# Zeroing the last blocks in 21 calls, and dense products in column groups, in a four-layer graph network on one core

## The chip, the cores and the metric

The kernel runs on one NeuronCore of a Trainium2 chip. The metric is the device time of one execution in microseconds. Before the change three executions gave a median of 3755.14 us (3753.14 to 3758.54).

The engines are TensorE (PE in the profile, with its weight loads as PEld), VectorE (DVE), ScalarE (ACT), GpSimd (POOL) and SyncE (SP, which starts most transfers). Sixteen DMA engines move the data.

## The reference

There are N = 6250 nodes with 128 features and E = 100000 edges. Four graph layers follow each other, each followed by a residual sum and a layer norm. All is float32.

```
agg0 = segment_sum(edge_attr, src) / max(count, 1)
x = layernorm(x + three_dense_layers_with_relu_and_batchnorm([x, agg0, u]))
x = layernorm(x + relu((segment_sum(x[src], dst) / max(deg, 1) + x) @ W1 + b1))
msg = [x[src], x[dst]] @ Wmsg[edge_type] + bmsg[edge_type]
h = [x, segment_sum(msg, dst) / max(count, 1)] @ Wupd + bupd
x = layernorm(x + (x + gelu(layernorm(h) * gamma2 + beta2)))
out3 = segment_sum(norm * (x @ W3)[row], col) + b3     # with self loops
x = layernorm(x + batchnorm(relu(out3)))
```

The two dense products of this study are `(agg + x) @ W1` of the second layer (layer 1) and `agg @ Wupd[128:]` of the third (layer 2).

## The kernel before

**Sorting the edges into blocks.** The nodes are cut into 49 groups of 128, so an edge belongs to one of 49 x 49 = 2401 pairs of groups. The kernel gives each pair blocks of four slots in a DRAM table, `slots`; a slot has 136 floats (128 features and 8 of payload), a block 544 floats, 2176 bytes. The last block of each pair may be part empty, so it is zeroed first. For this VectorE makes the list of the 2401 last blocks (`last_b`, 49 x 49), SyncE writes it to DRAM and reads it back as a table with one row to a lane, `zero_idx` (L556 to L561), and GpSimd issues 19 indirect transfers of zeros (L734), each with one column of the table, 128 lanes. Lanes without an entry hold a number out of bounds, and write nothing.

GpSimd then waits until all the zeros have landed, and scatters the edges: 782 indirect transfers (L750) of 128 edges each, 544 bytes to an edge. While it does that, TensorE, VectorE and ScalarE work out where each edge goes.

**The layers.** After the sort the kernel reads the slots back (`reduce`), gathers source rows (`gather`) and scatters them again, layer by layer. Each layer's sums over edges are matmuls with one-hot matrices (L1379, L1412, L1414, L1424). Between these long loops stand short stages on the nodes, in STEPS = 7 steps of STEP = 7 groups.

**The two stages of this study** are `f1` (layer 1) and `f2` (layer 2). A step of either goes in a ring over three engines. VectorE makes seven 128 x 128 operands in `zr` (L2065, L2141); TensorE turns them with seven transposes into PSUM (`turn`, L1465); ScalarE copies them to `zt` (L1004); TensorE multiplies each of the seven by the weights (`dense`, L1521); VectorE takes the products (L2072 and L2074 in `f1`, L2148 in `f2`). One PSUM area (banks 2 and 3) holds the products, so `dense` of a step waits until VectorE has taken those of the step before, and ScalarE's copy to `zt` waits for the `dense` before it. The program order on TensorE is written out by hand: turn of step i + 1, then dense of step i. In the second half of `f1`, TensorE does the messages of layer 2 between these steps (L1538, L1541).

In `dense` the turned nodes are the stationary operand (128 x 128) and the weights the moving one (128 columns). Each float32 matmul stands in the trace as two weight loads and two matmul records; a transpose stands as one of each.

Of the kernel before, what the change touches and what calls it, by code (L numbers as in the profile page):

```python
# [16 lines left out]
P = 128  # L17
# [7 lines left out]
STEPS = GROUPS // STEP  # L25
# [22 lines left out]
BLK = 4  # L48
# [70 lines left out]
ROW_A = D + PAY  # L119
ROW_G = D + 6  # L120
AW = D + 5
NOWHERE = 1.0e6
LASTB = 19
LASTP = GROUPS * GROUPS // LASTB
LASTN = GROUPS * GROUPS - LASTP * LASTB
assert LASTP < P and 0 < LASTN

HALF = STEP * P // 2
EPS = 1e-5
# [51 lines left out]
def gnn_kernel(nc, x, src, dst, edge_attr, edge_type, edge_weight, u, W0, b0, W1, b1, W2, b2,  # L181
               g0, bt0, g1, bt1, g2, bt2, L1W, L1b, Wmsg, bmsg, Wupd, bupd, gam2, bet2,
               W3, b3, gam3, bet3, out):
    with ExitStack() as ctx:
        def sb(name, shape, dt=F32):
            return ctx.enter_context(nc.sbuf_tensor(name, shape, dt))
# [4 lines left out]
        def dram(name, shape, dt=F32):  # L191
            return nc.dram_tensor(name, shape, dt).ap()

        slots = dram("slots", [NBLK, BLK * ROW_A])
# [14 lines left out]
        zt = sb("zt", [P, STEP, D])  # L209
# [73 lines left out]
        zeros = hot_raw[:, 0:BLK * BLK * ROW_A]  # L283
# [28 lines left out]
        last_b = sb("last_b", [GROUPS, GROUPS], U32)  # L312
        zero_idx = sb("zero_idx", [P, LASTB], U32)
        key_bc = pays_raw[:, COLS * PAY:COLS * PAY + ARING * CB * P // 2].bitcast(I16).rearrange(
# [35 lines left out]
        wT = sb("wT", [P, 6, D])  # L350
        wcat = sb("wcat", [P, 8, D])
# [100 lines left out]
        def tslot(j, base=0):  # L452
            return ps[:, base + j // 4, (j % 4) * D:(j % 4 + 1) * D]
# [40 lines left out]
        def turned_keys(k):  # L494
            return ps[0:KROWS, 3 + k, 0:CB * P // 2].bitcast(BF16).rearrange("p (q n) -> p q n", q=CB)
# [11 lines left out]
        def _(sp):  # L507
# [44 lines left out]
            for k, v in enumerate((bmsg[0], bmsg[1], bmsg[2], bupd, L1b)):  # L552
# [5 lines left out]
            flat = last_blocks.rearrange("a b -> (a b)")  # L558
            sp.dma_start(zero_idx[0:LASTP, :], flat[0:LASTP * LASTB].rearrange("(p k) -> p k", k=LASTB)).then_inc(
                last_out, 16)  # L560
            sp.dma_start(zero_idx[LASTP:LASTP + 1, 0:LASTN], flat[LASTP * LASTB:].rearrange(  # L561
                "(p k) -> p k", k=LASTN)).then_inc(last_out, 16)
# [127 lines left out]
        def _(pool):  # L690
# [39 lines left out]
            pool.sem_inc(issued, 1)  # L730
            pool.wait_ge(last_out, 48)
            pool.sem_inc(issued, 1)
            for k in range(LASTB):
                pool.indirect_dma_start(  # L734
                    slots, bass.IndirectOffsetOnAxis(zero_idx[:, k:k + 1], 0), zeros[:, 0:BLK * ROW_A], None,
                    bounds_check=NBLK - 1, oob_is_err=False).then_inc(last_zero, 16)
            pool.wait_ge(last_zero, 16 * LASTB)
            pool.sem_inc(issued, 1)
# [507 lines left out]
        def _(pe):  # L1246
# [14 lines left out]
            for k in range(2):  # L1261
                for q in range(CB):
                    ins = pe.transpose(turned_keys(k)[:, q, :], sg[:, k, q * KROWS:(q + 1) * KROWS], ident_h[:, :])
# [8 lines left out]
            for c in range(2):  # L1272
                ins = pe.matmul(ps[0:GROUPS, 7, 256:256 + GROUPS], ident[0:PAIR, c:PAIR:2], pair_sums[:, c:PAIR:2],
                                start=c == 0, stop=c == 1)
# [5 lines left out]
                      stop=True).then_inc(tables_turned, 1)  # L1280
# [50 lines left out]
            for k in range(2):  # L1331
                n = min(4, VECTORS - 4 * k) * D
                if k:
                    pe.wait_ge(prep_out, 6 + k)
                pe.matmul(bank(7, n), ones[0:1, :], bc_src[0:1, 4 * k * D:4 * k * D + n],
                          start=True, stop=True).then_inc(prep_t, 1)
# [20 lines left out]
            for k, b in ((0, 5), (1, 1)):  # L1357
                pe.matmul(bank(b, TILES), row128[0:GROUPS, 0:1].broadcast_to([GROUPS, P]), tile_on[:, k, :],
                          start=True, stop=True)
                pe.matmul(bank(b + 1, TILES), heads[:, 8 + k:9 + k].broadcast_to([GROUPS, P]), tile_on[:, k, :],  # L1360
                          start=True, stop=True)
                pe.matmul(bank(b + 2, TILES), ones[0:GROUPS, :], tile_on[:, k, :],
                          start=True, stop=True).then_inc(tile_done, 1)
# [97 lines left out]
            def turn(stage, i, operands=zr, base=0):  # L1461

                for j in range(STEP):
                    pe.wait_ge(st[stage]["z"], i * STEP + (j + 1))
                    ins = pe.transpose(tslot(j, base), operands[:, j, :], ident[:, :])  # L1465
                ins.then_inc(st[stage]["t"], 1)
# [24 lines left out]
            for k, stage in ((1, "mlp1"), (2, "mlp2")):  # L1491
                for n in range(2 * STEPS):
                    pe.wait_ge(bn_applied, (k - 1) * 2 * STEPS + n + 1)
                    pe.matmul(product_bank(stage, n), wT[:, 2 + k, :], A[:, n * HALF:(n + 1) * HALF],
                              start=True, stop=True).then_inc(st[stage]["m"], 1)
                if k == 1:
                    pe.wait_ge(lanes_ready, 3)
                    for v, table in enumerate((lanes, lanes_t)):
                        if v:
                            pe.wait_ge(lane_rows_made, v)  # L1500
                        for q in range(LTURNS):
                            ins = pe.transpose(lanes_turned[:, q, :], table[:, q * LCOLS:(q + 1) * LCOLS], ident_h[:, :])
# [11 lines left out]
            gather(1)  # L1514
            reduce(1)

            def dense(stage, w, i):

                pe.wait_ge(st[stage]["c"], i + 1)
                for j in range(STEP):  # L1520
                    ins = pe.matmul(tslot(j, 2), zt[:, j, :], w, start=True, stop=True)  # L1521
                ins.then_inc(st[stage]["m"], 1)


# [25 lines left out]
            def f1_dense(i):  # L1550
                if i:
                    pe.wait_ge(st["f1"]["r"], i)
                dense("f1", wT[:, 5, :], i)

            turn("f1", 0)
            f1_turn(1)
            f1_dense(0)
            f1_turn(2)
            f1_dense(1)
            f1_turn(3)  # L1560
            f1_dense(2)

            f1_dense(3)
# [28 lines left out]
            turn("f2", 0)  # L1592
            pe.wait_ge(st["f2"]["c"], 1)
            turn("f2", 1)
            dense("f2", wcat[:, 7, :], 0)
            with pe.Fori(1, STEPS - 1) as i:
                pe.wait_ge(st["f2"]["c"], i + 1)
                turn("f2", i + 1)
                pe.wait_ge(st["f2"]["r"], i)
                dense("f2", wcat[:, 7, :], i)  # L1600
            pe.wait_ge(st["f2"]["r"], STEPS - 1)
            dense("f2", wcat[:, 7, :], STEPS - 1)

            def z_turn(i):
                if i < CHUNKS[2][0]:
# [637 lines left out]
```

## Time and profile before

| | |
|---|---|
| median of the runs | 3755.14 us (3753.14 to 3758.54) |
| span of the profiled execution | 3754.1 us (the profile has no other time of that execution; the span lies 1.0 us under the median) |
| mean granted TensorE clock | 0.961 |
| busy: PE, DVE, POOL, ACT | 75%, 67%, 50%, 40% |
| chain that ended last | PE 39%, POOL 23%, issue 14%, DMA 12%, DVE 5%, ACT 3% |

In the chain, "issue" is time in which an engine waited for nothing that the profile shows. The share of busy time is a mean over stages that have different limits: GpSimd carries the chain while it scatters the edges (114 to 1103 us), TensorE in most of the rest. The stages `f1` (2063 to 2134 us, shared with the messages of layer 2) and `f2` (2999 to 3043 us) are short.

### The profile page before, as it was taken

What the parts mean: (1) busy time and instruction counts of PE and PEld (TensorE: products, weight loads), DVE (VectorE), ACT (ScalarE), POOL (GpSimd) and SP (SyncE); (2) the same over time, 40 slices, a digit from 0 to 9 for tenths busy, and PEclk for the clock granted to TensorE, in tenths of its full rate; (3) what the DMA queues carried; (4) which work ended last, traced back from release to release, by engine and by line L of the source; (5) the groups of instructions that cost most, each with busy time, mean ns of one, the idle gap of its engine ahead of it and who ended that gap; (6) DMA issues with size and microseconds to landing.
All of it is one profiled execution on the core that took longest, in us unless ns stands there. A gap on an engine that the chain in (4) does not pass through costs nothing.

```text
span 3754.1 us, 95326 instructions
## 1 busy us (share of the span) xinstructions
PE 2826.7 (75%) x23184; PEld 2448.4 (65%) x23185; DVE 2500.2 (67%) x7099; ACT 1518.9 (40%) x4337; POOL 1873.3 (50%) x2268
## 2 busy tenths in 40 slices
PE   8555544444439986778799799999999957777996
PEld 6232322222229965777799479999888957777995
DVE  7666666666647778555577777777666776554667
ACT  0111000000004445555576543222365347887665
POOL 4777777777763342777434344444432007774000
PEclk9999999999999998999899899999999969998998
DMA  6444444444449933888697035555477817786883
GB/s 214 151 149 144 146 149 141 149 143 147 148 130 290 291 128 118 279 275 277 221 290 255 9 127 180 173 183 177 136 226 235 263 38 269 275 275 197 286 281 122
DMA packets 419029, 721.55 MB, mean 192 GB/s; under 512 B 68624, under 2 KB 198169, under 8 KB 417932
## 3 DMA queue, kind: packets, MB, share of 16 engines
q1 hardware_dynamic: 330492, 494.35, 43.0%
q0 software_dynamic: 88464, 226.43, 16.0%
q14 instruction: 52, 0.43, 0.0%
q8 instruction: 21, 0.34, 0.0%
HBM read 481.26 MB, written 285.09 MB: 204 GB/s over the span
## 4 chain that ended last, share of the span: by engine, by line
PE 39%; POOL 23%; issue 14%; DMA 12%; DVE 5%; ACT 3%; SPq 2%; DVEq 1%; POOLq 1%; ACTq 0%
POOL slots L750 19%; PE ps L1379 18%; PE ps L1412 9%; DMA gbuf<-ring_raw,to_blk 8%; PE ps L1414 5%; POOL gbuf L804 4%; DMA ring_raw<-gbuf 3%; PE ps L1254 2%; PE ps L1465 1%; PE ps L1456 1%; SPq L501 1%; SPq L622 1%; DVE stats L1930 1%; PE ps L1521 1%; DVEq L501 1%
## 5 line engine op out<-in xcount | busy, mean ns | idle before, releaser
L804 POOL DMA_INDIRECT gbuf<-ring_raw,to_blk x774 | 754.2, 974 | 728.9 <-DVE ring_raw L1863 261.9
L750 POOL DMA_INDIRECT slots<-ring_raw,idx_edges x782 | 751.4, 961 | 242.3 <-issue 242.3
L1379 PE MATMUL ps<-ring_raw,memory 128*128 128x128 f32 (+2 forms) x6576 | 783.9, 279 | 84.9 <-DVE memory L1831 49.4
L1379 PEld LDWEIGHTS ps<-ring_raw,memory 128*128 128x128 f32 x6576 | 763.3, 192 | 113.1 <-issue 60.3
L1831 DVE TENSOR_TENSOR memory<-dst_lane,lane_ids 128x512 f32<-128x512 f32 x774 | 539.6, 698 | 73.3 <-POOL dst_lane L768 51.1
L1290 PE MATMUL ps<-memory 128*49 128x343 bf16 (+6 forms) x784 | 263.5, 489 | 387.9 <-DVE memory L1727 386.6
L1412 PE MATMUL ps<-memory 128*128 x2752 | 497.7, 273 | 10.2 <-DVE memory L1872 8.0
L1841 DVE TENSOR_TENSOR memory<-memory,ps 128x128 f32 (+2 forms) x1032 | 293.4, 284 | 314.7 <-PE ps L1379 302.6
L936 ACT ACTIVATE memory<-lane_ids,dst_lane 128x128 f32<-128x128 f32 x1032 | 331.0, 395 | 400.3 <-PE ps L1379 263.1
L1414 PE MATMUL ps<-memory 128*128 x2752 | 477.5, 220 | 0.0
L1290 PEld LDWEIGHTS ps<-memory 128*49 128x49 bf16 x784 | 113.9, 159 | 530.7 <-DVE memory L1727 301.9
L1424 PE MATMUL ps<-memory 128*128 x2064 | 270.2, 292 | 88.2 <-ACT ring_raw L977 49.9
L888 ACT COPY ring_raw<-memory 128x49 f32 (+1 forms) x112 | 26.0, 232 | 767.5 <-DMA slots<-ring_raw,idx_edges 767.4
L1424 PE MATMUL ps<-X,memory 128*128 x2064 | 267.0, 290 | 78.3 <-DVE memory L1886 31.0
L1424 PEld LDWEIGHTS ps<-memory 128*128 128x128 f32 x2064 | 255.8, 203 | 102.7 <-issue 101.3
L1424 PEld LDWEIGHTS ps<-X,memory 128*128 128x128 f32 x2064 | 252.8, 202 | 92.7 <-issue 91.8
L977 ACT ACTIVATE ring_raw<-ps,edge_w 128x128 f32<-128x128 f32 x1032 | 277.7, 407 | 68.9 <-issue 48.8
L1412 PEld LDWEIGHTS ps<-memory 128*128 128x128 bf16 x2752 | 269.8, 98 | 47.1 <-issue 15.2
L980 ACT COPY ring_raw<-ps 128x512 f32<-128x512 f32 x258 | 151.3, 586 | 361.9 <-PE ps L1414 361.9
L1863 DVE TENSOR_TENSOR ring_raw<-ring_raw,ps 128x512 f32<-128x512 f32 x258 | 177.5, 688 | 144.7 <-ACT ring_raw L980 144.7
L1414 PEld LDWEIGHTS ps<-memory 128*128 128x128 bf16 x2752 | 269.1, 98 | 2.4
L1886 DVE TENSOR_TENSOR memory<-memory,ps 128x512 f32<-128x512 bf16 x252 | 173.5, 689 | 112.4 <-PE ps L1424 112.4
(283 smaller groups left out, 4801.6 us busy)
## 6 DMA issues: line engine op xcount, KB each, us to landing
ring_raw<-gbuf SPq DMA_DIRECT2D x669, 268.0 KB, 3.7
ring_raw<-in_edge_attr SPq DMA_DIRECT2D x111, 448.0 KB
ring_raw<-slots SPq DMA_DIRECT2D x153, 272.0 KB, 4.0
zr<-lane_rows SPq DMA_DIRECT2D x87, 384.0 KB
zt<-lane_rows SPq DMA_DIRECT2D x87, 384.0 KB
memory<-lane_rows SPq DMA_DIRECT2D x84, 384.0 KB
memory<-slots SPq DMA_DIRECT2D x105, 272.0 KB, 4.0
memory<-gbuf SPq DMA_DIRECT2D x105, 268.0 KB, 3.8
```

The source lines that it names most:

```text
L750: pool.indirect_dma_start(edges, bass.IndirectOffsetOnAxis(idx_edges[0:n, u, j:j + 1], 0), edge_rows[0:n, u, j, :], None).then_inc(scatter ...
L804: pool.indirect_dma_start(gbuf, bass.IndirectOffsetOnAxis(to_blk[:, t:t + 1], 0), node_rows[:, r, :], None, bounds_check=NBLK - 1, oob_is_ ...
L936: ins = act.activation(hots[:, r, j * P:(j + 1) * P], lane_ids[:, :], ACT.Abs, bias=dst_lane[:, bass.ds(at, 1)], scale=-1.0)
L977: ins = act.activation(rows[:, j, 0:D], parts[:, j, :], ACT.Copy, scale=edge_w[:, bass.ds(at * BLK + j, 1)])
L1290: ins = pe.matmul(counts_of(s)[:, j * GROUPS:].rearrange("p (n g) -> p n g", g=GROUPS), hot2[:, u, 0, :, j], hot2[:, u, 1, :, j][:, None, ...
L1379: ins = pe.matmul(bank(r % 3, width), hots[:, r, j * P:(j + 1) * P], rows[:, j, 0:width], start=j == 0, stop=j == BLK - 1)
L1412: pe.matmul(to.rearrange("p (k d) -> p k d", d=D), hot, msgs[:, 0:2, bass.ds(at[r] + t * D, D)], start=t == 0, stop=False, skip_group_chec ...
L1414: ins = pe.matmul(to[:, D:2 * D], hot, msgs[:, 2, bass.ds(at[r] + t * D, D)], start=False, stop=t == TYPES - 1, skip_group_check=True)
L1424: ins = pe.matmul(bank(r)[:, j * P:(j + 1) * P], hots[:, r, j * P:(j + 1) * P], nodes[:, bass.ds(at[r], D)], start=True, stop=True)
L1831: dve.tensor_tensor(hots[:, r, :].rearrange("p (k d) -> p k d", d=P), lane.broadcast_to([P, BLK, P]), lane_ids[:, None, :].broadcast_to([P ...
L1841: dve.tensor_tensor(to, to, bank(r % 3, width), ALU.add).then_inc(added, 1)
L1863: dve.tensor_tensor(rows, rows, pair_bank(r)[:, :, 0:D], ALU.add).then_inc(staged, 1)
```

## The change

It has two parts.

The table of last blocks gets 21 columns in place of 19, and the 21 transfers have lane counts of their own, `ZERO_LANES`, from 115 to 128 (2563 lanes in all, where it was 19 x 128 = 2432). The entries fill 114 full rows and seven entries of one more, where it was 126 and seven, so every call has at least the lanes that hold entries. The number of blocks zeroed stays 2401.

In `dense` each 128 x 128 by 128 product is made in pieces: the stationary operand is cut by columns, which are the partitions of the result. `f1` makes two pieces of 64 columns, `f2` four of 32. Each piece goes to its own group of columns of the array and its own partitions of PSUM; the moving operand (128 columns) is passed again for each piece. The semaphore is still counted up by the last matmul of a step.

```diff
-LASTB = 19
+LASTB = 21
+ZERO_LANES = (128, 127, 126, 125, 124, 123, 122, 121, 120, 119, 118, 117, 116, 115, 127, 124, 120, 122, 126, 128, 115)
...
-assert LASTP < P and 0 < LASTN
+assert LASTP < min(ZERO_LANES) and 0 < LASTN and len(ZERO_LANES) == LASTB
...
-            for k in range(LASTB):
+            for k, n in enumerate(ZERO_LANES):
                 pool.indirect_dma_start(
-                    slots, bass.IndirectOffsetOnAxis(zero_idx[:, k:k + 1], 0), zeros[:, 0:BLK * ROW_A], None,
+                    slots, bass.IndirectOffsetOnAxis(zero_idx[0:n, k:k + 1], 0), zeros[0:n, 0:BLK * ROW_A], None,
                     bounds_check=NBLK - 1, oob_is_err=False).then_inc(last_zero, 16)
...
-            def dense(stage, w, i):
+            def dense(stage, w, i, span):
...
                 for j in range(STEP):
-                    ins = pe.matmul(tslot(j, 2), zt[:, j, :], w, start=True, stop=True)
+                    for b in range(0, P, span):
+                        ins = pe.matmul(tslot(j, 2)[b:b + span], zt[:, j, b:b + span], w, start=True, stop=True)
...
-                dense("f1", wT[:, 5, :], i)
+                dense("f1", wT[:, 5, :], i, P // 2)
...
-            dense("f2", wcat[:, 7, :], 0)
+            dense("f2", wcat[:, 7, :], 0, P // 4)
```

The other two calls of `dense` for `f2` change in the same way. How this stands in the program is shown for the three places that matter.

GpSimd's queue after the payload columns, before (DMA rows show the destination and the count):

```order
L727 TENSOR_SCALAR memory<-memory 128x784
L734 DMA slots<-memory,zero_idx 26928x544 x19
L754 UNCONDITIONAL_BRANCH
L754 ISA
L747 ISA
L750 DMA slots<-ring_raw,idx_edges 107712x136 x7
```

and now:

```order
L728 TENSOR_SCALAR memory<-memory 128x784
L735 DMA slots<-memory,zero_idx 26928x544 x21
L755 UNCONDITIONAL_BRANCH
L755 ISA
L748 ISA
L751 DMA slots<-ring_raw,idx_edges 107712x136 x7
```

Two transfers more stand ahead of the first scatter; nothing else moved.

TensorE's queue at the start of `f1`, before (`ident,zr` rows are the transposes, `wT,zt` rows the dense products, with partitions x columns of the result):

```order
L1465 MATMUL ps<-ident,zr 128x128 x14
L1521 MATMUL ps<-wT,zt 128x128 x7
L1465 MATMUL ps<-ident,zr 128x128 x7
L1521 MATMUL ps<-wT,zt 128x128 x7
L1465 MATMUL ps<-ident,zr 128x128 x7
L1521 MATMUL ps<-wT,zt 128x128 x14
```

and now:

```order
L1466 MATMUL ps<-ident,zr 128x128 x14
L1523 MATMUL ps<-wT,zt 64x128 x14
L1466 MATMUL ps<-ident,zr 128x128 x7
L1523 MATMUL ps<-wT,zt 64x128 x14
L1466 MATMUL ps<-ident,zr 128x128 x7
L1523 MATMUL ps<-wT,zt 64x128 x28
```

The order is the same; each dense product is two instructions, half as high.

TensorE's queue at the end of `f2`, before (`wcat,zt` rows are the dense products, `ident,memory` rows the next stage's transposes):

```order
L1465 MATMUL ps<-ident,zr 128x128
L1521 MATMUL ps<-wcat,zt 128x128 x7
L1596 REGISTER_ALU
L1596 COMPARE_AND_BRANCH
L1521 MATMUL ps<-wcat,zt 128x128 x7
L1614 MATMUL ps<-ident,memory 128x128 x14
```

and now:

```order
L1466 MATMUL ps<-ident,zr 128x128
L1523 MATMUL ps<-wcat,zt 32x128 x28
L1598 REGISTER_ALU
L1598 COMPARE_AND_BRANCH
L1523 MATMUL ps<-wcat,zt 32x128 x28
L1616 MATMUL ps<-ident,memory 128x128 x14
```

Here each product is four instructions, a quarter as high.

## Rows read from the trace of the kernel before

**Rows 1.** The page: chain that ended last, by engine and by line
```profile
PE 39%; POOL 23%; issue 14%; DMA 12%; DVE 5%; ACT 3%; SPq 2%; DVEq 1%; POOLq 1%; ACTq 0%
POOL slots L750 19%; PE ps L1379 18%; PE ps L1412 9%; DMA gbuf<-ring_raw,to_blk 8%; PE ps L1414 5%; POOL gbuf L804 4%; DMA ring_raw<-gbuf 3%; PE ps L1254 2%; PE ps L1465 1%; PE ps L1456 1%; SPq L501 1%; SPq L622 1%; DVE stats L1930 1%; PE ps L1521 1%; DVEq L501 1%
```

**Rows 2.** Timeline of POOL: start, length in us, instruction, [idle before]
```profile
85.14 1.21 POOL L734 DMA_INDIRECT slots<-memory,zero_idx  x1 [50.43 <-issue]
...
109.08 0.97 POOL L734 DMA_INDIRECT slots<-memory,zero_idx  x1 [0.30 <-issue]
114.01 0.96 POOL L750 DMA_INDIRECT slots<-ring_raw,idx_edges  x1 [3.96 <-issue]
...
1101.58 0.96 POOL L750 DMA_INDIRECT slots<-ring_raw,idx_edges  x1 [0.30 <-issue]
```

**Rows 3.** L734 and L750: count, min/median/max ns, first and last start
```profile
L734 POOL DMA_INDIRECT slots<-memory,zero_idx x19: 972/973/1356, 85.1 to 109.1; - x19
...
L750 POOL DMA_INDIRECT slots<-ring_raw,idx_edges x782: 879/958/1121, 114.0 to 1102.8; - x196
```

**Rows 4.** DMA queue row of the page; windows while zeroing (last columns: PEclk, DMA share, GB/s)
```profile
q0 software_dynamic: 88464, 226.43, 16.0%
...
90.00:95.00 5.00, 4.60 (x31) 2.79 (x30) 4.86 (x18) 0.57 (x2) 3.78 (x5) 1.00 0.90 278
...
110.00:114.00 4.00, 2.32 (x8) 1.06 (x9) 3.73 (x21) 0.00 (x0) 0.05 (x1) 1.00 0.20 74
```

**Rows 5.** L1521, matmuls: count, min/median/max ns, first and last start
```profile
L1521 PE MATMUL ps<-wT,zt x98: 272/275/533, 2068.8 to 2133.1; 128*128 128x128 f32 x98
...
L1521 PE MATMUL ps<-wcat,zt x98: 274/421/422, 3004.4 to 3041.7; 128*128 128x128 f32 x98
```

**Rows 6.** Timeline of PE in f1
```profile
2102.81 1.74 PE L1521 MATMUL ps<-wT,zt 128*128 128x128 f32 x14
2104.73 0.96 PE L1465 MATMUL ps<-ident,zr 128*128 128x128 f32 x7 [0.18 <-issue]
...
2118.05 2.69 PE L1465 MATMUL ps<-ident,ring_raw 128*128 128x128 f32 x7 [3.87 <-ACT ring_raw L1088]
...
2133.55 0.59 PE L1538 MATMUL ps<-wcat,ring_raw 128*128 128x384 f32 x1
```

**Rows 7.** Timeline of all engines in two steps of f2
```profile
3009.00 2.05 PE L1465 MATMUL ps<-ident,zr 128*128 128x128 f32 x7 [1.44 <-DVE zr L2141]
...
3010.84 2.36 PE L1521 MATMUL ps<-wcat,zt 128*128 128x128 f32 x14
...
3013.24 1.09 DVE L2148 TENSOR_TENSOR memory<-ps,memory 128x896 f32<-128x896 f32 x1 [1.36 <-PE ps L1521]
...
3029.51 3.19 PE L1521 MATMUL ps<-wcat,zt 128*128 128x128 f32 x14
```

**Rows 8.** Windows of single steps (PE, PEld, DVE, ACT, POOL busy; PEclk, DMA, GB/s)
```profile
2071.20:2078.00 6.80, 4.12 (x21) 3.53 (x21) 5.41 (x17) 0.93 (x2) 0.00 (x0) 0.75 0.00 0
...
2990.00:2999.90 9.90, 8.70 (x74) 8.18 (x72) 5.62 (x18) 2.00 (x5) 0.00 (x0) 1.00 0.53 172
...
3007.60:3013.20 5.60, 4.20 (x21) 3.53 (x21) 4.28 (x15) 0.90 (x1) 0.00 (x0) 0.59 0.00 0
...
3032.70:3039.00 6.30, 4.80 (x22) 3.76 (x21) 5.16 (x22) 1.24 (x3) 0.00 (x0) 0.77 0.00 0
```

**Rows 9.** Groups by form: stationary size, moving size, count, busy us, mean ns
```profile
L1254 PE MATMUL ps<-memory 128*128 128x98 bf16 x392 | 61.7, 336 | 0.3 <-DVE memory L1666 0.3
...
L1290 PE MATMUL ps<-memory 128*49 128x98 bf16 x112 | 37.3, 333 | 0.0
```

**Rows 10.** Timeline at the end of f2
```profile
3040.57 8.19 ACT L1066 ACTIVATE memory<-memory,nmr,rstd 128x128 f32<-128x128 f32 x21 [0.69 <-DVEq L2153]
...
3045.30 0.17 DVE L1949 SCALAR_TENSOR_TENSOR mv<-mv,sd 128x14 f32<-128x14 f32 x1
...
3048.67 0.29 ACT L1054 ACTIVATE sd<-mv,eps_col 128x14 f32<-128x14 f32 x1
```

More of the change, by code:

```diff
@@ L1599, in _ @@
                 pe.wait_ge(st["f2"]["r"], i)
-                dense("f2", wcat[:, 7, :], i)
+                dense("f2", wcat[:, 7, :], i, P // 4)
             pe.wait_ge(st["f2"]["r"], STEPS - 1)
-            dense("f2", wcat[:, 7, :], STEPS - 1)
+            dense("f2", wcat[:, 7, :], STEPS - 1, P // 4)
             def z_turn(i):
```

## The prediction, made before the changed kernel was timed

> **What bounds the kernel now.** I read the chain of waits first. It says who carries the end: TensorE 39%, GpSimd 23%, and by line the scatter L750 alone 19%, while the dense line L1521 has 1% [rows 1]. So one edit sits in front of the longest GpSimd stage, and the other in a line that is small but on the chain.
>
> Then the timeline of GpSimd around the zeroing. Its 19 calls run from 85.14 us, the last starts at 109.08, and the first scatter starts at 114.01, after 3.96 us in which GpSimd waits for the zeros to land [rows 2]. From there to 1101.58 every scatter has only the 0.30 us of issue before it, and the row of the line gives 782 calls with a median of 958 ns [rows 2, 3]: 782 x (0.958 + 0.30) is 984 us, the whole stretch from 114 to 1103. GpSimd never waits in it, so whatever delays the first scatter delays the end by the same amount. Nothing covers it.
>
> Then the two node stages, by timeline and windows. A step of `f2` is a ring: seven transposes, dense, VectorE's L2148, the next operands, the transposes again [rows 7]. Dense (3010.84 to 3013.20) is followed at 3013.24 by L2148, which waited for it; the next transposes wait for VectorE. So dense stands in the ring with nothing beside it. TensorE's clock changes between its two levels there: steps have a granted clock of 0.59 to 0.77 against 1.00 in the loop before, where TensorE was busy 8.70 us of 9.90; in the steps it is busy 4.20 of 5.60 and 4.80 of 6.30 [rows 8].
>
> **The zeroing.** A call costs 0.973 us and 0.30 between calls, 1.27 us [rows 2, 3]. Two more calls: +2.55 us. Fewer lanes make a call cheaper: the last scatter has 32 lanes and is the minimum of its line, 879 ns against 958 at 128 lanes [rows 3], 0.8 ns a lane. The mean lane count goes from 128 to 122, so 21 calls save 21 x 6 x 0.8 ns = 0.1 us. Sum +2.45 us. The bytes stay the same (2401 blocks), and the last landing comes behind the last call as before, if the blocks of a call are spread over the DMA engines as evenly as now. If lanes cost nothing it is 2.55; if odd counts take another path on GpSimd, no row shows it. The list's reload has 114 rows of 21 entries for 126 of 19, the same 9.4 KB; I cost that at nothing, within 0.3 us either way.
>
> The other end is uneven spreading. The GpSimd queue moved 226.43 MB in 16.0% of 16 engines' span [rows 4]: 9611 engine-microseconds, 23.6 GB/s for one engine. A call of 127 lanes carries 114 blocks of 2176 bytes, 0.25 MB: 0.7 us over sixteen engines, 10.5 us on one. The fifteenth call has 127 lanes and is issued six calls, 7.7 us, before the last; on one engine its zeros land some 3 us after the last call's would, and the calls behind it queue on top. DMA engines were already 0.90 busy from 90 to 95 us and only 0.20 in the last four [rows 4], so there is room only at the end. I price this end at +4 us on top of the 2.5, with 2 to 8 as its bounds. I take the even spreading, because all the transfers in the trace so far cost what a spread one would.
>
> The Trainium skill speaks against this edit ("DMA: Bandwidth & Descriptors", section "Why a DMA increments its semaphore by 16 and not by 1"): a DMA uses the largest number of engines up to 16 that divides its slowest dimension, so 128 partitions use 16 and 127 only one, though it says that some transfers issued from GpSimd are spread anyway. The kernel before has only 128 and 32 lanes in its indirect transfers, so no row of it tests this. By the rule the zeroing costs about 6.5 us, without it 2.45.
>
> **The dense products.** A dense step is 14 matmul records. At the full clock 14 of them take 1.74 us with a last one of 0.27 [rows 5, 6]: 0.113 us from one to the next. At the low clock 14 take 3.19 with a last one of 0.42 [rows 5, 7]: 0.213 us. The moving operand stays 128 columns long for each piece. Do narrower results make a matmul shorter? The same 98 moving columns took 333 ns with 49 stationary columns and 336 with 128 [rows 9]. So a piece costs what a whole product does, unless pieces in different column groups run beside each other. No row has two groups, so I bound it from both sides.
>
> - Nothing overlaps: `f1` 28 records for 14, `f2` 56 for 14. Added per step 14 x 0.113 = 1.6 us in `f1` and 42 x 0.113 = 4.7 us in `f2`; at the low clock 3.0 and 8.9.
> - All pieces of a product overlap: added 0.
> - The middle, which I take: the engine starts matmuls in program order, and a piece is two records in the same columns, which must follow each other. The second record of a piece can run beside the first of the next piece, in other columns. Then a piece costs one record time. `f1`: 14 pieces, as now. `f2`: 28 pieces, 14 more record times, +1.6 us a step at the full clock and +3.0 at the low one.
>
> The nearest rows [rows 9] would give the first end; but they are all in one group and say nothing of two, which is why I go to the middle and keep both ends in the range.
>
> The Trainium skill ("TensorE: Matmul & The Clock Gate", section "Part 3: Packing small matmuls — row/col tiling") says that matmuls in different column groups run concurrently, while they start and end in strict program order; three groups gave 2.38 times the throughput. By it the first bound is too dear, and the middle one is what order and two records a product leave. By rows 9 alone the sum would be the serial one below.
>
> How many steps count: in `f2` the seventh dense does not. Behind it ScalarE is busy for 8.19 us from 3040.57, while the variances that hang on that dense are ready at 3045.47 and are taken at 3048.67 [rows 10]: 3.2 us of cover. Six steps count. In `f1` the sixth dense is followed by 3.87 us of idle TensorE, waiting for ScalarE [rows 6], so it is covered too; the seventh is not (next matmul 2133.55 directly behind it). Six again.
>
> The clock: the ring's low share falls as TensorE gets busier. At a granted clock of about 0.7 the mean record time is some 0.17 us, and 14 more are +2.4 us a step. If half of the low time goes, 28 records take 28 x 0.143 = 4.0 us against 2.4 now, +1.6, and the transposes, 2.05 us at the low clock [rows 7] and 0.96 at the full one [rows 6], give back some 0.4. That is +1.2 a step, x6 = +7 us; with no gain of the clock +14, with all of it +3. I take +8. Changing between whole and cut arrays twice a step may cost something; I put 0.5 us for both stages.
>
> Sum: 2.45 + 8 + 0.5 = +11 us, from a span of 3754.1 to 3765.1. The median of the runs is 1.0 above that span, so 3766.1 us.
>
> **Rivals.**
> - *Serial pieces.* For it: rows 9. Twelve steps: 6 x 4.7 + 6 x 1.6 = 37.8 us at the full clock, less some 16 that transposes and old records gain if the clock stays full: +22; at the clock as it stands 6 x 7.2 + 6 x 2.0 = +55. Middle +38, with the zeroing +40: 3795 us (3779 to 3812).
> - *Full overlap.* TensorE's time unchanged, only the zeroing: 3757.6 us, or 3761.5 with the uneven one.
> - *Uneven spreading* comes on top of any case, chance 0.35, +4 us. Against it: nothing but the missing row.
> - *The clock, on the other side.* If pieces overlap fully and their denser stream holds the clock at its full level through both stages, a ring step of `f2` is 0.96 for the transposes, 1.74 dense and 1.4 for VectorE, 4.1 us for the 5.6 to 6.9 of now: about -2.1 x 6, and -1.5 x 3 in the first steps of `f1`, whose window at 0.75 has a third of its time low. With +2.5 for the zeroing, 3741 us. It decides from the point where both stages stay at 1.00. Against it: the gap of some 1.4 us in each step stays.
> - *The change does nothing to the stream*, if pieces were merged: the order shows 14 and 28 instructions, so no.
>
> **How the numbers follow.** Middle overlap 0.42 (its own range 3759 to 3777), serial 0.32, full overlap 0.18, clock gain 0.08. A change of under 0.2%, 7.5 us, can't be told from none. Same (3747.6 to 3762.6): most of the full overlap (0.16), a fifth of the middle (0.09), a little of the clock's (0.02): 0.27. Faster: 0.05. Slower: 0.68. The range leaves out the clock's case below and the dearest third of the serial case above: 3755 to 3804.
>
> **What would show it.** Zeroing: 21 calls of 0.97 us, and the wait before the first scatter still 3.96 us, the scatter starting at about 116.5; a wait of 6 us or more means uneven spreading. If lanes cost more than now, calls differ in length. Dense: in `f1` 28 records in 1.7 us at the full clock, in `f2` 56 records in 3.3 us and not 6.4 or 1.7; starts of records in pairs. The clock windows of `f2` at about 0.85. I am wrong if record starts are 0.11 us apart throughout (serial), or if `f2` takes no longer than now.

## The result, and the profile after

The changed kernel took 3779.74 us (median of three, 3776.12 to 3780.36) against 3755.14: a ratio of 1.0063 [1.0043, 1.0083], 24.6 us slower. The profiled execution has a span of 3778.6 us (3754.1 before) and a granted clock of 0.964 (0.961 before). The prediction was 3766.1 us, in a range of 3755 to 3804. The direction and the range hold. The working does not: +11 us was meant as 2.45 for the zeroing and 8 for the dense products. It was 20.5 (e2, below) to 23.5 for the zeroing, by the start of the first scatter, and for the dense products nothing that the runs can tell. (In the runs below, one execution of e10, 13838 us, and one of the kernel before beside e10, e11 and e12, 5426 us, were slow ones: the ratios leave them out, and without it e10's median is 3772.15 us and not 3774.16.)

**Where the trace moved.** I laid the two traces over each other and took the start of the same instruction in both. On VectorE the difference is 0.1 us until 85 us; from 124 us to the end of the edge scatter (1100 us) it stands between 23.4 and 23.6 us, and at 2055 us it is 23.8. Over the stage `f1` it grows to 30.3, over `f2` it changes by under 1 us, and in layer 3 (3100 to 3750 us) some 6 us come back, so that 24.5 are left at the end. So the time is lost in one place, between 85 and 137 us.

The chain of the page has the same owners as before [rows 1], and the page's row of GpSimd's DMA queue has 4752 packets more for nearly the same bytes (0.04 MB more) [rows 4]:

```profile
PE 40%; POOL 23%; issue 13%; DMA 12%; DVE 4%; ACT 3%; SPq 2%; DVEq 1%; POOLq 1%; ACTq 0%
...
q0 software_dynamic: 93216, 226.47, 16.2%
```

**The zeroing.** GpSimd's timeline, with the same columns as [rows 2]. The lane counts of these rows are, in order, 128, 127, 126, 125, 124, 123, 122, 121, and after the gap 127, then the last call with 115, and the first scatter:

```profile
85.29 1.22 POOL L735 DMA_INDIRECT slots<-memory,zero_idx  x1 [50.47 <-issue]
86.81 2.87 POOL L735 DMA_INDIRECT slots<-memory,zero_idx  x1 [0.30 <-issue]
89.98 1.02 POOL L735 DMA_INDIRECT slots<-memory,zero_idx  x1 [0.30 <-issue]
91.30 1.19 POOL L735 DMA_INDIRECT slots<-memory,zero_idx  x1 [0.30 <-issue]
92.80 1.58 POOL L735 DMA_INDIRECT slots<-memory,zero_idx  x1 [0.30 <-issue]
94.68 1.42 POOL L735 DMA_INDIRECT slots<-memory,zero_idx  x1 [0.30 <-issue]
96.40 1.67 POOL L735 DMA_INDIRECT slots<-memory,zero_idx  x1 [0.30 <-issue]
98.38 1.01 POOL L735 DMA_INDIRECT slots<-memory,zero_idx  x1 [0.30 <-issue]
...
108.75 2.57 POOL L735 DMA_INDIRECT slots<-memory,zero_idx  x1 [0.30 <-issue]
...
119.26 1.17 POOL L735 DMA_INDIRECT slots<-memory,zero_idx  x1 [0.30 <-issue]
137.46 0.98 POOL L751 DMA_INDIRECT slots<-ring_raw,idx_edges  x1 [17.02 <-issue]
```

Two losses can be read here. The calls are no longer of one length: 127 lanes take 2.87 and 2.57 us, 122 take 1.67, 126 and 121 still 1.0. From the first call's start to the last one's end it is 35.1 us (85.29 to 120.43), where it was 24.9 (85.14 to 110.05): +10.2. And then GpSimd waits 17.0 us for the zeros, where it was 3.96: +13.0. The rest is the 0.15 us by which the first call starts later.

While GpSimd waits, nobody else works. The first two windows are those of [rows 4]; the third is the wait:

```profile
90.00:95.00 5.00, 4.70 (x31) 2.79 (x30) 4.86 (x19) 0.57 (x2) 4.09 (x4) 1.00 0.58 132
110.00:114.00 4.00, 1.71 (x4) 0.70 (x5) 3.75 (x17) 0.00 (x0) 3.39 (x3) 1.00 0.60 120
120.00:137.00 17.00, 0.00 (x0) 0.00 (x0) 0.00 (x0) 0.00 (x0) 0.43 (x1) 1.00 0.32 73
```

From 90 to 95 us the DMA engines moved 132 GB/s at a busy share of 0.58; before it was 278 at 0.90. The work that was done early before is still under way after the last call. The queue's row for the time from the first call to the first scatter, before and after, and the same row of e6 (21 calls of 127 lanes, below):

```profile
q0 software_dynamic: 1520, 5.23, 44.1%
...
q0 software_dynamic: 6272, 5.26, 46.3%
...
q0 software_dynamic: 21840, 5.39, 31.2%
```

All the packets that came on top belong to the zeroing, and they are tiny: 20320 more of them in e6 carry 0.16 MB more, 8 bytes each.

**The dense products.** TensorE's rows in `f1` and `f2`, to be held against [rows 5 to 7]:

```profile
2092.61 3.26 PE L1523 MATMUL ps<-wT,zt 128*64 128x128 f32 x28
...
2130.86 1.75 PE L1523 MATMUL ps<-wT,zt 128*64 128x128 f32 x28
...
3034.38 1.74 PE L1523 MATMUL ps<-wcat,zt 128*32 128x128 f32 x56
...
3039.57 2.97 PE L1523 MATMUL ps<-wcat,zt 128*32 128x128 f32 x56
...
3046.01 3.16 PE L1523 MATMUL ps<-wcat,zt 128*32 128x128 f32 x56
```

At the full clock 56 records of four groups take 1.74 us, and 28 records of two groups 1.75; before, 14 records took 1.74 [rows 6]. A single record is not shorter (the median of the `wcat` records is 421 ns, as in [rows 5]). So four stand beside each other throughout: read one by one in e1's trace, the records of a step at the full clock start in fours, 6 to 7 ns apart, and most fours start 109 to 110 ns after the one before; before the change one record started every 111 to 112 ns. At the low clock 56 records take 3.16, and 14 took 3.19 [rows 7].

### The profile page after: what moved, and what is told of

It reads as the page before. It is cut to its first block, busy times and chain, and to the rows that moved or that the text cites. A ratio compares the mean times of both kernels' runs of the same rounds, so it can differ in the third digit from the quotient of the medians.

```text
span 3778.6 us, 96114 instructions
## 1 busy us (share of the span) xinstructions
PE 2829.5 (75%) x23576; PEld 2440.7 (65%) x23577; DVE 2502.3 (66%) x7099; ACT 1521.7 (40%) x4337; POOL 1881.9 (50%) x2270
## 3 DMA queue, kind: packets, MB, share of 16 engines
q0 software_dynamic: 93216, 226.47, 16.2%
## 4 chain that ended last, share of the span: by engine, by line
PE 40%; POOL 23%; issue 13%; DMA 12%; DVE 4%; ACT 3%; SPq 2%; DVEq 1%; POOLq 1%; ACTq 0%
POOL slots L751 19%; PE ps L1380 18%; PE ps L1413 9%; DMA gbuf<-ring_raw,to_blk 8%; PE ps L1415 5%; POOL gbuf L805 3%; DMA ring_raw<-gbuf 3%; PE ps L1255 2%; PE ps L1425 1%; PE ps L1466 1%; PE ps L1457 1%; SPq L502 1%; PE ps L1523 1%; ACT ring_raw L978 1%; SPq L623 1%
## 5 line engine op out<-in xcount | busy, mean ns | idle before, releaser
L1425 PE MATMUL ps<-memory 128*128 x2064 | 268.4, 289 | 86.1 <-ACT ring_raw L978 42.1
```

The lines of the kernel that those rows point to most:

```text
L1425: ins = pe.matmul(bank(r)[:, j * P:(j + 1) * P], hots[:, r, j * P:(j + 1) * P], nodes[:, bass.ds(at[r], D)], start=True, stop=True)
```

## The experiments

The theory after reading the trace: the lane counts slow the zeroing through the number of DMA engines that share a call, and the dense products cost nothing. Its rivals: part of the loss comes from the dense products, or from the two extra calls as such, or odd lane counts are slow for another reason; and, on the wait alone, that one late transfer makes it. All kernels keep the program of the kernel after, but for the edit shown. Each was timed against the kernel before on its own chip (medians of before: 3757.15, 3755.40 and 3757.23 us). e6 and e11 have two executions each and e12 has three; the others have four to eleven.

### The two parts apart

```diff
# e1: only the dense products in column groups
+LASTB = 19
+ZERO_LANES = (P,) * LASTB
# e2: only the 21 calls of mixed lane counts
+    ins = pe.matmul(tslot(j, 2), zt[:, j, :], w, start=True, stop=True)
```

> Zeroing as before (19 calls of 128 lanes), dense in 2 and 4 column groups as changed. Theory: pieces in different column groups overlap fully, 14, 28 and 56 records all take 1.74 us at the full clock, so only the change between whole and cut arrays costs, 0.1 to 0.3 us a step: 0 to +5 us on the median of before, 3755 to 3760. First scatter at 114.0 us. Rival: the 6 us by which the changed kernel's f1 stage was longer are the pieces' own cost and stay: +6 us or more. Rival of the prediction (half overlap): +8.

> The 21 calls of 115 to 128 lanes, dense whole as before. Theory: the lane counts are all of the loss. First scatter at 137.5 us as in the changed kernel, time +23.5 us, 3778 to 3779. Rival: the dense pieces carry 6 us or more of the 24.6, then this run is under 3774.

e1: 3756.98 us, ratio 0.9997 [0.9986, 1.0007]. e2: 3774.41 us, 1.0048 [1.0033, 1.0064]. The loss is in the zeroing. The parts make -0.2 and +17.3 us, the whole 24.6; their intervals (12 to 24 us for e2, 16 to 31 for the kernel after) overlap. In e2 GpSimd's first scatter starts 20.5 us later than before, in the kernel after 23.5; the calls have the same lengths, and the difference is the wait (13.85 and 17.02 us), which so differs between two executions of the same zeroing. Timelines of GpSimd, e1 and e2:

```profile
113.61 0.96 POOL L751 DMA_INDIRECT slots<-ring_raw,idx_edges  x1 [3.64 <-issue]
```

```profile
134.49 0.98 POOL L751 DMA_INDIRECT slots<-ring_raw,idx_edges  x1 [13.85 <-issue]
```

### Two more calls, nothing else

```diff
# e3: dense products whole, and
+ZERO_LANES = (P,) * LASTB     # 21 calls of 128
```

> 21 calls, all of 128 lanes (entries in 114 rows and seven as in the changed kernel), dense whole. Theory: the number of calls costs 2 x 1.27 = 2.5 us and nothing else: first scatter at 116.6 us, wait before it 4 us, 3757.7. Rival: lanes without an entry, or the shorter table, cost: then the wait before the first scatter is well over 4 us.

3757.58 us, 1.0005 [0.9996, 1.0014]. The first scatter starts at 116.05, 2.0 us later than before [rows 2], the median call is 972 ns. So my +2.45 us would have been about right for two calls more of 128 lanes: the calls added 2.6 us, and the wait was 3.07 us for 3.96.

### The order of the mixed calls

```diff
# e4: same counts, dense products whole, those that share few engines first
+ZERO_LANES = (127, 127, 122, 118, 122, 123, 124, 116, 124, 125, 115, 115, 119, 121, 117, 126, 126, 120, 120, 128, 128)
```

> The same 21 lane counts as the changed kernel in another order: those whose largest divisor up to 16 is small first (127, 127, 122, 118, 122, 123, ...), those of 120, 126 and 128 last. Dense whole. Theory: a call uses as many DMA engines as that divisor. GpSimd's calls take as long in sum (35 us), but the slow transfers drain beside later calls, so the wait before the first scatter falls from 17 us to 4 to 8: first scatter at 125 to 129 us, time +11 to +15. Rival: the wait of 17 us comes from the number of lanes or bytes alone, then it stays.

3774.97 us, 1.0053 [1.0038, 1.0069]: no better than e2. The wait fell only from 13.85 to 12.25 us, not to the 4 to 8 that I expected. That is what the rival on record would give, a wait from the number of lanes or bytes alone; but e3 above, with more lanes and the same bytes, waits only 3.07 us. So it is neither that nor one late transfer at the end, but a backlog that the calls with few engines leave whatever their order. Its windows (columns as in [rows 8]) show few bytes moved at the start, and the engines catching up when the well divided calls come:

```profile
85.00:95.00 10.00, 8.19 (x58) 5.14 (x56) 9.45 (x37) 1.59 (x5) 8.51 (x4) 1.00 0.42 96
95.00:105.00 10.00, 7.34 (x52) 4.62 (x52) 9.72 (x44) 1.14 (x4) 8.17 (x7) 1.00 0.60 140
105.00:115.00 10.00, 5.12 (x35) 3.01 (x33) 9.51 (x36) 0.44 (x1) 7.87 (x8) 1.00 0.89 159
115.00:120.00 5.00, 2.98 (x26) 2.03 (x24) 4.00 (x15) 0.00 (x0) 3.78 (x5) 1.00 0.93 202
120.00:125.00 5.00, 0.00 (x0) 0.00 (x0) 0.00 (x0) 0.00 (x0) 0.73 (x1) 1.00 0.81 244
```

### One lane count for all 21 calls

```diff
# e5, e6, e9, e11, e12: dense products whole, and
+ZERO_LANES = (126,) * LASTB     # 127, 120, 122, 124
```

> 21 calls, all of 126 lanes, dense whole. 126 is no multiple of 16; its largest divisor up to 16 is 14. Theory (as many DMA engines as that divisor): 14 engines of 9 lanes each, calls of 1.0 us, wait before the first scatter 4 to 5 us, first scatter at 117 to 119 us, +3 to +5. Rival (any count that is no multiple of 16 takes a slow path): calls over 1.1 us or a wait of 12 us and more, +15 and up.

> 21 calls, all of 120 lanes, dense whole. Largest divisor up to 16: 15, eight lanes each. Theory: as with 126 lanes, calls of 1.0 us, wait 4 to 5 us, +3 to +4. Rival (multiples of 16 only are fast): as dear as the changed kernel.

> 21 calls, all of 127 lanes, dense whole. Theory: one DMA engine a call, another for each; calls of 2.6 to 2.9 us as the two of 127 lanes in the changed kernel, 21 x 3.1 = 65 us, then 10 to 12 us for the last 0.25 MB on one engine: first scatter at about 161 us, +47, 3802. Rival (cost grows with the mixture of counts only): calls near 1 us, first scatter before 125.

> All 21 calls with 122 lanes (largest divisor up to 16: two); dense products whole. The divisor theory: every call 1.66 us, calls over at 85 + 21 x 1.96 = 126.5 us, then a wait between that of 120 and 126 lanes (4) and that of 127 (16): about 8 us, first scatter at 135, time about 3776 us. If only odd counts are slow, 122 lanes are as 126: 3758 us.

> All 21 calls with 124 lanes (largest divisor up to 16: four); dense products whole. The divisor theory: every call 1.31 us, calls over at 85 + 21 x 1.61 = 119 us, a wait of about 5 us, first scatter at 124, time about 3765 us. If a call's length or landing doesn't hang on the divisor, as 126 lanes: 3758 us.

Call and first scatter come from the rows of the two lines, packets from the page's queue row; "to scatter" is from the first call's start to the first scatter's.

| lanes | largest divisor up to 16 | lanes over it | median call, us | to scatter, us | packets of q0 | time, us, and ratio |
|---|---|---|---|---|---|---|
| 128 (e3) | 16 | 8 | 0.972 | 30.6 | 88624 | 3757.58, 1.0005 [0.9996, 1.0014] |
| 120 (e9) | 15 | 8 | 1.000 | 31.7 | 88624 | 3757.38, 1.0012 [1.0001, 1.0022] |
| 126 (e5) | 14 | 9 | 0.990 | 32.4 | 88960 | 3758.32, 1.0007 [0.9997, 1.0016] |
| 124 (e12) | 4 | 31 | 1.314 | 42.6 | 92656 | 3773.99, 1.0039 [1.0022, 1.0056] |
| 122 (e11) | 2 | 61 | 1.671 | 70.4 | 97696 | 3797.52, 1.0108 [1.0086, 1.013] |
| 127 (e6) | 1 | 127 | 2.547 | 110.4 | 108784 | 3834.96, 1.0215 [1.0194, 1.0235] |

Neither the count nor whether it is odd orders this table. The third column does, down to 120 and 126 lanes, which differ by 1% in the call: 124 lanes are far slower than 120, and 127 than 126. e5 and e9 cost about what e3 does. e12 came out above what I had written (a wait of 7.7 us for 5, and a time 9 us higher), and e11 and e6 more so, by some 20 and 30 us. Most of those two misses stands in GpSimd's timeline. e6, where the lines are the 8th and the 15th call and the first scatter:

```profile
124.85 2.55 POOL L735 DMA_INDIRECT slots<-memory,zero_idx  x1 [18.43 <-issue]
...
160.62 2.54 POOL L735 DMA_INDIRECT slots<-memory,zero_idx  x1 [16.12 <-issue]
...
196.14 0.99 POOL L751 DMA_INDIRECT slots<-ring_raw,idx_edges  x1 [15.88 <-issue]
```

and e11, its 16th and 17th call and the first scatter:

```profile
115.97 1.67 POOL L735 DMA_INDIRECT slots<-memory,zero_idx  x1 [0.30 <-issue]
133.41 1.67 POOL L735 DMA_INDIRECT slots<-memory,zero_idx  x1 [15.77 <-issue]
...
155.97 0.99 POOL L751 DMA_INDIRECT slots<-ring_raw,idx_edges  x1 [13.00 <-issue]
```

GpSimd stalls in the middle of the zeroing, with 127 lanes after every 7 calls and with 122 after 16. In lanes per engine that is 7 x 127 = 889 (an eighth would make 1016) and 16 x 61 = 976 (a 17th would make 1037). Neither the kernel after nor e12 has such a stall; their sums are 725 and 651. In e6 the stall lasts until the engines have nearly run dry: their busy share is 0.06 from 120 to 125 us. One reading is that a queue has room for about a thousand entries; it was not tested, since no run changes anything else.

### Without the two calls of 127

```diff
# e10: the mixed counts, dense products whole, but
-... 127, ..., 127, ...
+... 126, ..., 126, ...
```

> The mixed lane counts of the change, but both calls of 127 lanes made 126; dense products whole. Theory A: the two calls that go to one DMA engine are what lands last, and the calls with 2 to 5 engines cost mostly GpSimd's time. Then the calls take 2 x 1.75 us less (calls over at about 117), the wait before the first scatter falls from 13.9 to 4 to 7 us, and the time is 3761 to 3767 us against 3774 with both 127. Theory B: the backlog comes from all calls with few engines; the wait stays at 10 to 13 us and the time is 3768 to 3772 us.

3774.16 us (3772.15 without the one of 13838 us), 1.0045 [1.0028, 1.0062], with a wait of 12.71 us: on the side of the backlog, Theory B. The two one-engine calls were the dearest, but the first scatter comes only 4.1 us earlier than in e2 (130.44 for 134.49), most of it GpSimd's shorter calls, and the interval of the time lies on e2's.

### Neighbours in the same column group

```diff
# e7: zeroing as before; in dense, the loops exchanged
-for j in range(STEP):
-    for b in range(0, P, span):
+for b in range(0, P, span):
+    for j in range(STEP):
```

> Zeroing as before. Dense in the same 2 and 4 column groups with the two loops exchanged: first all seven products' pieces of group 0, then all of group 1, and so on, so that neighbours in the queue are in the same columns. Theory: pieces overlap only when neighbours in the queue are in different columns. Now they can't: 28 records take 2 x 1.7 and 56 records 4 x 1.6 = 6.3 us at the full clock, first counted +1.6 and +4.7 a step in six steps of each stage; +25 to +45 us, 3782 to 3802. Rival: the chip reorders, or narrow pieces are short in themselves (a piece of 32 columns costs a quarter of a whole product in any order): 56 records still take 1.74 us and the time is that of before.

3786.04 us, 1.0083 [1.0067, 1.01]. The same 56 small products, in another order. Steps of `f2` in its timeline, with e1's under them:

```profile
3027.51 6.72 PE L1523 MATMUL ps<-wcat,zt 128*32 128x128 f32 x56
...
3068.07 5.08 PE L1523 MATMUL ps<-wcat,zt 128*32 128x128 f32 x56
```

```profile
3011.46 1.74 PE L1523 MATMUL ps<-wcat,zt 128*32 128x128 f32 x56
...
3016.64 2.87 PE L1523 MATMUL ps<-wcat,zt 128*32 128x128 f32 x56
```

Of e7's step at 3068 the window says that all of it lies at the full clock, which makes 1.74 us the row to compare:

```profile
3068.10:3073.10 5.00, 5.00 (x57) 4.79 (x56) 1.89 (x12) 0.31 (x1) 0.00 (x0) 1.00 0.00 0
```

The trace also shows what happens where one group's products end and the next group's begin. Two windows of that step, the first inside a group, the second at the first change of groups (the number behind PE's busy time counts the records that touch the window):

```profile
3068.50:3068.90 0.40, 0.40 (x6) 0.40 (x5) 0.40 (x4) 0.00 (x0) 0.00 (x0) 1.00 0.00 0
3069.19:3069.59 0.40, 0.40 (x10) 0.40 (x9) 0.39 (x3) 0.00 (x0) 0.00 (x0) 1.00 0.00 0
```

Inside a group one record starts every 109 ns. At the change, two such rows of starts run into each other: the first four records of the new group start between the last four of the old one. (The trace does not name a record's group; this is read from the spacing.) The overlap exists only between neighbours in the instruction stream that lie in different column groups, and in this order it reaches over about four records. Without it the dense products would have cost some 31 us by the ratio, and the serial rival had +38.

## Why the prediction was right and wrong

**That the first scatter sets the end** held: GpSimd's first scatter starts 23.45 us later than before and its last one 23.5, and VectorE's shift stays between 23.4 and 23.6 us up to 1100 us.

**The zeroing, +2.45 us: this step failed.** The sentence that failed is "if the blocks of a call are spread over the DMA engines as evenly as now", which I took because all transfers of the trace had been spread. They had 128 or 32 lanes, so they could say nothing on other counts. Uneven spreading had a chance of 0.35 and was what happened. The Trainium skill's rule ("DMA: Bandwidth & Descriptors", section "Why a DMA increments its semaphore by 16 and not by 1": the largest number of engines up to 16 that divides the slowest dimension) is borne out by the table: the order of its rows is that of this divisor. The exception that the Trainium skill allows there is for some direct copies issued from GpSimd; these transfers are indirect, and they follow the rule.

The packets tell it most sharply. In the six uniform kernels a call adds 16 x (h + 1) packets to a base of 86944 (all other packets of the queue: the 88464 of [rows 4], less 19 x 80, and 1520 is just what the row above has for the zeroing), where h is half of the lanes over the divisor, rounded up: 8 gives 80 a call, 9 gives 96, 31 gives 272, 61 gives 512, 127 gives 1040. For the mixed counts that makes 392 x 16 = 6272, so 93216, and for e10 274 x 16 = 4384, so 91328. The page of the kernel after has 93216, that of e10 this:

```profile
q0 software_dynamic: 91328, 226.45, 16.3%
```

Both agree to the packet, so the count of each call goes by this divisor in a program that mixes lane counts as well. The profile does not name the engines of a call; that the blocks are shared out by the divisor is inferred from these counts, the lengths of the calls and the times.

**The rival's price, +4 us on top (bounds 2 to 8), failed too**, and by more: it was 21 (18 in e2). Two things were missing from it. GpSimd's own time per call grows with the lanes of an engine: 0.972 us at 8, 1.314 at 31, 1.671 at 61, 2.547 at 127, or 13 to 15 ns for each lane beyond 8. Over the 21 mixed calls that is 557 such lanes, some 7.4 us at 13.2 ns, and with the two extra calls at 1.27 us some 9.9 of the measured 10.2. I had looked only at the landing. And I priced the landing as that of one late call of 127 lanes behind full engines. e4 and e10 show that neither its place nor its presence matters much. A mean does better: if every mixed call counted 1/21 of its uniform kernel's time to the scatter (110.4, 70.4 and 42.6 us for 1, 2 and 4 engines; put between them 55, 40 and 36 for 3, 5 and 7, and 31.5 for the eight others), the sum is 49 us. e2 has 49.0 (85.46 to 134.49), the kernel after 52.2. It is an estimate with three values interpolated, and the agreement may be chance: 110.4 and 70.4 hold the stalls in the middle, some 34 and 15 us, which no mixed kernel has. Without them the sum is 43. For e10 it gives 41 with them, and 45.1 was measured. How large the backlog of a mixture is, no run explains.

**The dense products, +8 us: this step failed**, in the other direction. e1 costs nothing that can be told, within -5 and +3 us by its interval. The step was "a piece is two records in the same columns, which must follow each other". In its place the runs show that the two records of a float32 matmul don't stop its neighbours in other groups: 56 records take the 1.74 us of 14. That was the full overlap, chance 0.18. The Trainium skill's sentence that column groups run concurrently ("TensorE: Matmul & The Clock Gate", section "Part 3: Packing small matmuls — row/col tiling") agrees; what I added to it from the strict order of starts and ends did not. My serial bound was right for neighbours in one group: inside a group e7's records start 0.109 us apart, where I had 0.113, and a record takes 273 ns with 32 stationary columns and 275 with 128, so the reading of [rows 9] held. That 56 records took 5.08 us and not 1.74 + 4.7 = 6.4 is the overlap at the three changes of groups, which neither bound had. The starts that interleave there also speak against the strict program order on which I built the middle. The +0.5 us for changing between whole and cut arrays is inside e1's interval, too small to be told.

**The clock.** I had expected windows of `f2` at about 0.85 because TensorE would be busier. It was not (busy 32.57 us of 43.0 in the kernel after, 32.08 of 42.1 before), and the granted clock over the same windows is 0.80 after and 0.72 before, with no time gained: the stage from its first transposes (3030.20) to the last dense product's end takes 42.2 us, before 42.0. In e7, where TensorE is busy 50.99 us of 60 in `f2`, it is 0.88. The rival of the clock's gain (3741 us) did not happen.

**`f1` in the profile.** The stage is 6 to 7 us longer in the kernel after and in e1, where steps at the start take 3.26 us for the 2.32 of before. That looks like a price of the split. e3, with whole products, shows it too:

```profile
2072.85 3.20 PE L1522 MATMUL ps<-wT,zt 128*128 128x128 f32 x14
2080.47 3.19 PE L1522 MATMUL ps<-wT,zt 128*128 128x128 f32 x14
```

Over `f1` the shift of VectorE's instructions grows from 2.2 to 9.0 us in e3, from 0.3 to 7.4 in e1, and from 20.3 to 23.6 in e2. So it is no cost of the split: it comes with whole products too, and in e1 the whole took what it took before. The steps of 3.2 us lie wholly at the low level of the clock (granted 0.50 over them, against 0.72 to 0.73 over the same two steps before), which falls on other steps in another execution; that this makes all of the 7 us was not shown. Where layer 3 gives it back I did not find out.

**The sum.** The forecast was 8 us too high for the dense products and 21 too low for the zeroing, which left 13 us between forecast and result. That the errors partly cancelled was luck. The range held because it was made wide for the serial rival, and that had nothing to do with the loss. The seventh dense product of `f2`, which I took as covered by 3.2 us, was tested by e7: it takes 5.08 us there for 1.83, 3.25 more, and ScalarE's use of the variances comes only 0.1 us later against the start of its long row (3074.79 to 3082.97, before 3040.57 to 3048.67 [rows 10]). So that reading held.

**Left open.** Whether the backlog comes from the blocks lying on few engines or from the thousands of tiny packets, which no run separates; why the engines move fewer bytes for their busy share when calls are unevenly divided (132 GB/s at 0.58 against 278 at 0.90); why the wait differs by 3 us between e2 and the kernel after; and what the stall after 7 and 16 calls is. No kernel here beats the one before: e1 equals it, and all kernels with 21 calls start the scatter later.

## What to carry to other kernels

Keep the partition count of an indirect transfer a multiple of 16 (128 is the one run here), or at least one with a large divisor up to 16 (126 and 120 were as good within 2 us), and pad with lanes that write nothing instead of cutting them off: 128 lanes cost 0.972 us a call and 127 cost 2.547, though both write the same 114 or 115 blocks. When a trace has only one shape of an operation, it is no evidence for another shape; a rule that says so deserves its full price, on the engine that issues as well as on the queue that carries. Small matmuls in different column groups run beside each other when neighbours in the stream alternate between groups: the same 56 took 1.74 us in that order and 5.08 group by group.

## What the runs showed of the hardware that I had not expected

- The time of an indirect transfer on GpSimd grows with the lanes that fall to one DMA engine by the divisor rule, from 0.972 us (8) to 2.547 us (127).
- The packets of a call grow with the lanes of its fullest engine: 80 with 8 lanes an engine, 1040 with 127. The added ones carry some 8 bytes each.
- GpSimd stalls 15.8 to 18.4 us in the middle of a series of such calls: after 7 calls with one engine, after 16 with two.
- Four column groups of float32 products overlap fully (56 records in 1.74 us), though each is two records; with seven products of one group in a row the same 56 take 5.08 us, and only about four records overlap where the group changes.
